# A relational graph convolution on one core: tiles of 125 edges in place of 128, a ring of 100 slots, gathers in groups of five

## The reference

```python
W = einsum('rb,bio->rio', comp, basis)             # one 128x128 matrix per edge type
msgs = einsum('ni,rio->nro', h, W)[src, et]
mean = segment_sum(msgs, dst*8 + et) / max(count, 1)
h = relu(mean.sum(over the 8 types) + h @ root + bias) + h
```

## Time and profile before

| | before |
|---|---|
| median of 3 runs | 5828.9 us (5816.82 to 5843.13) |
| the profiled execution's own time | 5821.83 us |
| its span, first to last instruction | 5819.8 us |
| PE busy | 3311.0 us (57%) |
| PEld busy | 2993.7 us (51%) |
| POOL busy | 3021.2 us (52%) |
| ACT busy | 2193.9 us (38%) |
| DVE busy | 1752.0 us (30%) |
| granted TensorE clock, mean | 0.757 of full speed |

### The profile page before, as it was taken

The page is one execution under the profiler, slowest core; times in us unless marked ns, Lnnn a source line. Parts: engine busy times, 40 slices in busy tenths (PEclk is TensorE's granted clock), DMA queues, the critical chain, the costliest instruction groups (busy, mean ns, idle before and its releaser), DMA issues. The chain is left out here.

```text
span 5819.8 us, 86058 instructions
## 1 busy us (share of the span) xinstructions
PE 3311.0 (57%) x19913; PEld 2993.7 (51%) x19913; DVE 1752.0 (30%) x6354; ACT 2193.9 (38%) x6238; POOL 3021.2 (52%) x3190
## 2 busy tenths in 40 slices
PE   0555555555555556555653556556555565555567
PEld 0445555555555555555632555555555455555557
DVE  3632222222222223222321222223222222222236
ACT  0443333333333333333531333333333333333346
POOL 7055555555555555555255555555555555555542
PEclk9877777777777777677875777777777777777789
DMA  3211111111111111111021111111111111111113
GB/s 77 49 48 39 39 36 38 37 38 38 38 39 39 37 39 39 38 38 38 18 74 42 39 39 36 38 39 38 39 39 39 38 36 39 38 39 38 39 28 89
DMA packets 170897, 239.76 MB, mean 41 GB/s; under 512 B 68942, under 2 KB 119340, under 8 KB 170726
## 3 DMA queue, kind: packets, MB, share of 16 engines
q0 software_dynamic: 100944, 207.56, 13.6%
q10 hardware_dynamic: 32098, 15.69, 1.1%
q1 hardware_dynamic: 37809, 15.99, 1.1%
HBM read 224.59 MB, written 14.44 MB: 41 GB/s over the span
## 5 line engine op out<-in xcount | busy, mean ns | idle before, releaser
L671 PE MATMUL bank<-S,W 128*128 128x128 f32 x9376 | 1577.7, 316 | 1240.9 <-issue 1234.4
L660 PE MATMUL bank<-onehot,rows 128*128 128x128 f32 x9376 | 1689.7, 332 | 1016.7 <-issue 693.0
L660 PEld LDWEIGHTS bank<-onehot,rows 128*128 128x128 f32 x9376 | 1488.3, 238 | 1224.6 <-issue 946.8
L671 PEld LDWEIGHTS bank<-S,W 128*128 128x128 f32 x9376 | 1439.3, 230 | 1301.0 <-issue 1290.8
L297 POOL DMA_INDIRECT ring<-h_rows,idx x1512 | 1426.4, 943 | 1158.1 <-SPq L399 709.7
L297 POOL DMA_INDIRECT ring<-x,idx x1512 | 1429.3, 945 | 1137.0 <-SPq L399 705.5
L521 ACT ACTIVATE rows<-ring,relnorm 128x128 f32 x4688 | 1503.5, 390 | 1119.7 <-issue 769.9
L503 ACT ACTIVATE S<-bank 128x512 f32<-128x512 f32 x1172 | 680.6, 581 | 2204.7 <-remote 2170.2
L850 DVE TENSOR_TENSOR onehot<-bank,relnorm 128x512 f32<-128x512 f32 x1172 | 810.2, 692 | 2034.6 <-issue 1555.1
L860 DVE TENSOR_TENSOR aggT<-aggT,bank 128x16 f32 x4688 | 792.9, 169 | 1861.1 <-remote 942.8
L345 POOL TENSOR_SCALAR aggT<-aggT 128x512 f32<-128x512 f32 (+1 forms) x17 | 27.8, 1636 | 238.1 <-DVE aggT L860 238.1
(11 more groups left out here) (113 smaller groups left out, 593.6 us busy)
## 6 DMA issues: line engine op xcount, KB each, us to landing
ring<-x,idx POOLq DMA_INDIRECT x1512
ring<-h_rows,idx POOLq DMA_INDIRECT x1512
S<-x ACTq DMA_DIRECT2D x24, 256.0 KB, 3.3
h_rows<-S SPq DMA_DIRECT2D x24, 256.0 KB, 3.0
onehot<-x ACTq DMA_DIRECT2D x24, 256.0 KB, 3.2
out<-S SPq DMA_DIRECT2D x24, 256.0 KB, 3.1
pairs<-aggT ACTq DMA_DIRECT2D x1, 1562.5 KB
idx<-srcT SPq DMA_DIRECT2D x56, 27.0 KB
```

The costliest lines, as they stand in the source:

```text
L660: last = t.matmul(bank[2 * (u % 2) + k // 4][:, k % 4 * P:(k % 4 + 1) * P], rows[:, at, :], onehot[:, at, :], start=True, stop=True)
L671: last = t.matmul(bank[4 + u % PB][:, 0:BATCH * WIN], W[:, L.n, r * H:(r + 1) * H], S[:, u % 2, :].rearrange("p (k r n) -> p k r n", r=REL ...
```

## The change: what it does

`R` = 125 edges make a tile. Since 200,000 = 1600 x 125 and 1600 = 16 x 100, there is no short tile, no rest after the rounds, and `idx_rest`, `src_tail` and `pad_pair` go with the code that used them. The ring has 100 slots, the groups are of five, and `FLIGHT` is 10, two groups in place of three. `LAG` = RING - FLIGHT stays 90. The steps are at most 1600 + 781 = 2381, so there are 298 batches. A gather, the scaling (L521) and the first matmul (L660) work on 125 partitions; the one-hot matrix is still made on 128.

```diff
-    TILES = -(-E // P)
+    R = 125
+    TILES = E // R
-    RING = 108
+    RING = 100
-    FLIGHT = 18
-    GROUP = 6
+    FLIGHT = 10
+    GROUP = 5
-    pairs = nc.dram_tensor("pairs", (TILES, 2 * P), F32).ap()
+    pairs = nc.dram_tensor("pairs", (TILES, 2 * R), F32).ap()
-    OFF0 = 15
+    OFF0 = 13
             def gather(L, table, slot, index):
-                g.indirect_dma_start(out=ring[:, slot * P:(slot + 1) * P], out_offset=None, in_=table,
+                g.indirect_dma_start(out=ring[0:R, slot * P:(slot + 1) * P], out_offset=None, in_=table,
...
-                    gather(L, table, slot, idx[:, slot // HALF, slot % HALF:slot % HALF + 1])
+                    gather(L, table, slot, idx[0:R, slot // HALF, slot % HALF:slot % HALF + 1])
...
                 with pool.Fori(1, ROUNDS) as t:
                     turn(L, table, t)
-                pool.wait_ge(rest_in, 32)
-                for slot in range(REST):
-                    if slot % GROUP == 0:
-                        pool.wait_ge(L.landed, ROUNDS * RING + slot + GROUP - FLIGHT)
-                    gather(L, table, slot, idx_rest[:, slot:slot + 1])
...
-                        tile_step[bass.ds(i - LAG + 16, FLIGHT), :].rearrange("(k g) a -> a k g", g=GROUP)[:, :, GROUP - 1],
+                        tile_step[bass.ds(i - LAG + OFF0 + 1, FLIGHT), :].rearrange("(k g) a -> a k g", g=GROUP)[:, :, GROUP - 1],
...
-                for i in range(0, REST, FLIGHT):
-                    pass_on(L, ROUNDS * RING + i, min(FLIGHT, REST - i), True, 16 * ((ROUNDS * RING + i) // FLIGHT + 1))
...
-                    s.activation(rows[:, u % 2 * BATCH + k, :], ring[:, bass.ds(v[2 * k + 1], P)], ACT.Copy,
-                                 scale=relnorm[:, 1, bass.ds(b * BATCH + k, 1)]).then_inc(L.weighted, 1)
+                    s.activation(rows[0:R, u % 2 * BATCH + k, :], ring[0:R, bass.ds(v[2 * k + 1], P)], ACT.Copy,
+                                 scale=relnorm[0:R, 1, bass.ds(b * BATCH + k, 1)]).then_inc(L.weighted, 1)
...
-                    last = t.matmul(bank[2 * (u % 2) + k // 4][:, k % 4 * P:(k % 4 + 1) * P], rows[:, at, :],
-                                    onehot[:, at, :], start=True, stop=True)
+                    last = t.matmul(bank[2 * (u % 2) + k // 4][:, k % 4 * P:(k % 4 + 1) * P], rows[0:R, at, :],
+                                    onehot[0:R, at, :], start=True, stop=True)
```

More of the change, by code:

```diff
@@ L13, with build @@
 TRUE_BY_SCHEDULE = "the schedule on the chip takes them from counts of tiles and windows, bounded by the shapes"
-def build(nc, x, srcT, src_tail, dst, et, basis, comp, root, bias, out):
+def build(nc, x, srcT, dst, et, basis, comp, root, bias, out):
     N, H = x.shape
@@ L26, in build @@
     GROUPS = -(-BATCHES * BATCH // P)
-    RING = 108
+    RING = 100
     HALF = RING // 2
-    FLIGHT = 18
-    GROUP = 6
+    FLIGHT = 10
+    GROUP = 5
     LAG = RING - FLIGHT
     ROUNDS = TILES // RING
-    REST = TILES - ROUNDS * RING
-    assert REST <= HALF and ROUNDS >= 4 and HALF % FLIGHT == 0
+    assert ROUNDS * RING == TILES and ROUNDS >= 4 and HALF % FLIGHT == 0
     ROWS = 125
     COLS = E // ROWS
-    BLK = COLS // 64
-    assert ROWS * COLS == E and COLS % 64 == 0 and E % 64 == 0
+    PART = 25
+    HB = R // PART
+    assert ROWS * COLS == E and COLS % PART == 0 and R % PART == 0
     TROWS = -(-TILES // P)
@@ L285, in _ @@
             g = nc.gpsimd
-            g.memset(idx_rest[:], 0)
             g.memset(ones[:], 1.0)
@@ L329, in _ @@
                             pool.wait_ge(rel_made, k - TB + 1)
-                        g.indirect_dma_start(out=pair_in[:, k % TB].rearrange("p b t k -> p (b t k)"), out_offset=None,
+                        g.indirect_dma_start(out=pair_in[:, k % TB].rearrange("p h t k -> p (h t k)"), out_offset=None,
                                              in_=pairs, in_offset=bass.IndirectOffsetOnAxis(ap=idxg[:, k:k + 1], axis=0)
@@ L361, in nodes_at @@
                 def nodes_at(first, rows, cols, to):
-                    span = dst[first:first + rows * cols * P].rearrange("(t j k) -> t j k", j=cols, k=P)
+                    span = dst[first:first + rows * cols * R].rearrange("(t j k) -> t j k", j=cols, k=R)
                     sp.dma_start(to, span[:, :, 0]).then_inc(tiles_in, 16)
@@ L731, in _ @@
             dve.sem_inc(cleared, 1)
-            v.memset(pad_pair[:, 0, :], -1.0)
-            v.memset(pad_pair[:, 1, :], 0.0)
             v.memset(epsc[:], EPS)
@@ L902 @@
     src = np.asarray(src)
-    full = src.shape[0] // P * P
+    rows = 125
     arrays = {
         "x": np.asarray(x),
-        "srcT": np.ascontiguousarray(src[:full].reshape(-1, P).T),
-        "src_tail": np.ascontiguousarray(src[full:]),
+        "srcT": np.ascontiguousarray(src.reshape(-1, rows).T),
         "dst": np.asarray(dst), "et": np.asarray(edge_type_8),
```

62 lines of the change are left out of this document (27 added, 35 removed).

## The result

The changed kernel takes 5071.5 us (median of four runs, 5070.35 to 5074.77) against 5827.6 us of the kernel before in the same comparison: a ratio of 0.870, 95% interval 0.869 to 0.872. I had forecast 5840 us, and 5700 to 6200 us as the range of eight in ten. The profiled execution is one of 5070.35 us with a span of 5068.2 us.

A forecast was written before the change was run, and what follows sets the result against it. No engine was the bound: GpSimd's gathers ran in chains, stopped by a consumer slow only during a stall. Terms 49 + 37 - 11 - 11 - 18 - 35 = +11 us gave 5833, forecast as 5840 us; eight-in-ten range 5700 to 6200.

The forecast's parts named there:

- the sum's ground: Both layers' gather loops: chains shorten from 12 gathers to 10, at 1.70 us per tile; +49 and +37 us.
- the stall: Stretch with single matmuls 1.43 us apart, from 7.5 us after a chain's first gather to 2.3 us after its last.
- chains of ten: Unbroken rows of GpSimd gathers, two groups of five, then a stop of 4.4 us; 1.665 us per tile without longer chains.
- The term of the gather: GpSimd's 3200 gathers of 125 rows: each shorter or unchanged, 0 to -70 us, taken as -35 us.
- By rows: A gather's 0.944 us scales with its rows: 125/128 saves 22 ns, 3200 times, -70 us.
- fixed: A gather's 0.944 us does not depend on its rows: 125 rows save nothing.
- The gather gets dearer: Rival, GpSimd's gathers: five engines, 36 packets for 32, stall longer, +300 us, 6140 us; chance 0.22.
- The stall shrinks: Rival, layer loops: shorter chains or fewer engines weaken the stall, 5500 us; -1340 us with no stall; chance 0.13.
- The smaller ring: 100 slots for 108: setup -11, layer 2's first chain -11, using up the ring after the last gathers -18 us.
- SyncE too late: Rival, SyncE's passing of slots: its read holds up a chain's third group, 6140 to 6440 us; chance 0.10.
- The number of engines: Gather's DMA: by the skill's rule 125 rows go to five engines, 25 rows each, at least 36 packets for 32.

The follow-up runs named there:

- the fifth comparison: With the stall, against the kernel before (5828.3 us): 128 rows with a memset behind each gather 5792.6 us; the changed kernel with bounded waits 5075.2 us.
- the first comparison: Without the stall, against the kernel before (4116.2 us): bounded waits 4117.6, changed kernel with bounded waits 5069.0, 125 rows alone 4938.4, ring of 96 with groups of four 4174.9 us.
- the second: Comparison with the stall, against the kernel before (5922.9 us): memset and drain behind each gather 10603 us; gathers of 120 rows 5905.9 us.
- the four others at 1.31 us and less: Kernel before with 64 rows (5931 us), 120 rows (5906), ring of 96 with groups of four and eight in flight (5846), or a memset behind each gather (5793).
- the four at 1.61 us and more: Kernel before with, behind each gather, a max over 64 columns (5343 us), over 96 columns (5602), two memsets (6341), or memset and drain (10603).

## Why the prediction was wrong

**The step that failed is the sum's ground: that the stall belongs to every chain and only the chains' length moves.** I priced the change as chains of ten with the same 7.5 us before the stall, 1.70 us per tile. There are no chains: the stall is gone, and a tile costs GpSimd's own 1.51 us. The rows had what was needed to doubt it. All engines but GpSimd slowed down while gathers came 1.25 us apart, and nothing in the profile held them. I called this a fact to be taken from the trace and did not ask what it would do if the gathers' pace changed. That the profile showed nothing to hold the engines up said less than I took it for, with most of its semaphore records missing.

**The term of the gather was wrong in sign.** I took -35 us, between 0 and -70. It is +0.27 us (1.21 less 0.94) for each of 3200 gathers, +860 us. By itself that makes the kernel slower, as it does where there is no stall: 4117 us become 5069 us, which is these 860 and 74 more gathers of 1.25 us. The bounds were no bounds. "By rows" and "fixed" were both drawn from one size, and the price is by the number in another way: 64, 120 and 128 rows cost 0.91 to 0.98 us and 32 packets, 125 rows cost 1.21 us and 80.

**The two rivals each had half of it.** "The gather gets dearer" (0.22) had the right event, but 36 packets in place of 80, and the wrong effect: I let the dearer gather lengthen the stall, 6140 us. Its 20 packets with rows are right, the small ones are 60 and not 16. "The stall shrinks" (0.13) had the right effect, with -1340 us if it goes, but from shorter chains. Together they come near: my 5840 less 1340 plus 860 is 5360, and the missing 290 us are mostly the setup's 76 (I had 11) and the two full rings' 200 (I had 18), which hung on the stall too. With the measured price of the stall the sum closes: 5828 less 1711 (5828 to 4117, the kernel before with and without it) plus 864 (3200 x 0.27) plus 92 (74 x 1.25) is 5073, for 5071 measured. I had no case in which one cause does both.

**The smaller ring, -11, -11 and -18.** The setup became 76 us shorter, not 11, by the stall's end. The use-up of the ring after the last gather fell by 100 us a layer, not 9: it goes by how far behind the consumer is, not by the number of slots. The ring with groups of four by itself gave 0.987 with the stall and 1.014 without. So on their own ring, groups and flight are of a small size, as I had them; that they are worth some 170 us together with the 125 rows (the fifth comparison) I did not see.

**SyncE too late** (0.10) did not happen. SyncE waits for the gathers' data for 1268.4 of 1800 us (1477.5 in the trace of the first comparison, which has its records whole), and GpSimd in that stretch never for SyncE.

**The number of engines.** No view names the engine of a packet, but the trace has each packet's start, length and size. A gather of 125 rows has 15 packets of eight rows (4096 bytes), 5 of one row (512 bytes) and 60 of 32 or 4 bytes. From 500 to 2300 us, for 97% of the time that packets of 4096 bytes are under way, there are at most five at once, while with 128 rows there are up to 16 and with 120 rows up to 15. By the rule of the Trainium skill that the prediction cites ("DMA: Bandwidth & Descriptors", "Why a DMA increments its semaphore by 16 and not by 1"), 125 rows go to five engines and 120 rows to 15. The trace agrees: five times three packets of eight rows and one of one row are the 125. So the prediction's step to five engines was right, and what it had wrong was the price.

**What is shown and what is not.** Shown: 125 rows alone end most of the stall (5912 to 5135 us), ring and groups alone don't (5846 us), and 128 rows in the old form lose it when they come 1.61 us apart or more. That it is the pace and not the form of the 125-row gather that ends it is the simplest reading of these, not shown for 1.51 us itself. Since one program has the stall in one comparison and not in the next, a variant could also have missed it by chance; but where the kernel before had it, the four others at 1.31 us and less had it too, and none of the four at 1.61 us and more did.

Open: why the consumer of 125 rows alone still falls a ring behind in the old ring and that of the whole change doesn't; and why the kernel before has the stall in one comparison and not in another. On one and the same chip it took 4116 us in the first and 5923 us in the second. It had none in the two comparisons with four kernels beside it and had it in the five with two and in that of the result, which may point to something of how programs lie in memory, but no run separates that.

What a gather hands to the other engines so that they crawl is open too. The lost records point to the recording: where the records are whole, 64, 125 and 128 rows leave as many of them for their landings (53,082, 53,093 and 52,946 for 3126 gathers and the rest), which is in line with 64 rows having the stall like 128, and the loss and the stall come in the same comparisons. The Trainium skill ("NOTIFIC — the notification-queue block", "7.1 Overflow: three behaviours, one of which stalls the engine") says that the block that writes the engines' records does one of three things when the ring for them is full: it discards new ones, overwrites old ones, or holds the producer up until software has drained the ring. The first and the last of these would fit records that are missing and engines slowed alike without a semaphore in sight, and would make the stall, and with it the change's 13%, a matter of being profiled. It is not shown: every run here has its span and clock from a recording, so no run tells the time without one.

## What to carry to other kernels

When several engines slow down together and the profile names no releaser, look for what runs at the same time on another one, and vary its pace before you vary anything else: here an added operation on GpSimd made the kernel 8% faster, where it had the stall. Measure the kernel before again whenever you measure a variant; it moved by over 40% between comparisons, and the same change was 13% faster in one and 23% slower in the next. Count the trace's records of semaphores against those of a trace that is whole before you believe in a stall without a releaser. And price a gather at the very number of rows that it will have: 125 are dearer than 128, 120 and 64.

## What the runs showed of the hardware that I had not expected

- A gather of 512-byte rows by GpSimd takes 0.945 us for 128 rows, 0.98 us for 120, 0.91 to 0.95 us for 64, with 32 packets each, but 1.21 us and 80 packets for 125.
- With gathers of 64 to 128 rows 1.21 to 1.31 us apart, the other engines can fall to single instructions some 0.7 to 3.5 us apart, in the loops some 7.5 us after the first of a row of gathers; with gathers 1.61 us and more apart they did not, and with 125 rows every 1.51 us only in part, in the old ring. Traces of the runs at 1.31 us and less that had it have under a third of their semaphore records.
- A gather of 125 rows has at most five of its eight-row packets under way at once for 97% of the time, one of 128 rows up to 16, one of 120 rows up to 15.
- With a memset and a drain behind a gather, GpSimd sits idle for 2.2 us before the next; a memset that waits for the one before costs 0.06 to 0.10 us of GpSimd's pace (1.31 us in a row and 1.35 us on the mean, for 1.25 us).
- A gather that comes 0.17 us behind a max over 128x64 or 128x96 on GpSimd took 1.03 us in place of 0.95 us; 0.17 us behind a memset of 128x96 it took 0.95 us.
